# A vision tower on one core: the first group's images loaded at once, pads filled in the opening, maxima spread by one product, the first down integers by two engines, and new orders of work

## The reference

```python
# tokens: quantised patch embedding
xn  = x * rsqrt(mean(x*x) + 1e-6)                       # per patch
xq  = round(xn * s) / s,  s = 127 / clip(max|xn|, 1e-5)
wq  = clip(round(w / clip(mean|w|, 1e-5)), -1, 1) * mean|w|
h   = concat([cls, xq @ wq.T]) + pos                    # (64, 50, 256)

# attention: three sets of weights on the same normed input, 16 heads of 16, causal
for i in range(3):
    q, k, v = (layernorm(h) @ W.T + b for W, b in ((Wq[i], bq[i]), (Wk[i], bk[i]), (Wv[i], bv[i])))
    w = exp(s - max(s)),  s = q @ k.T * 4 with a causal mask
    o = (w / (sum(w) + 1e-6)) @ v @ Wo[i].T + bo[i]
    out[i] = layernorm(o, ln_g[i], ln_b[i])
h = h + layernorm(concat(out) @ Wout.T + bout, ln2_g, ln2_b)

# feed-forward with integers; both maxima run over the WHOLE tensor
y     = layernorm(h);  sx = sigmoid(clip_x) * max|y| / 127
gate  = round(y / sx) * sx @ wq(w_gate).T;  up = the same with w_up   # 704 wide
a     = silu(gate) * up;  sa = sigmoid(clip_down) * max|a| / 127
h     = h + clip(round(a / sa)) * sa @ wq(w_down).T
```

## Time and profile before

| what | value |
|---|---|
| median of 3 runs | 772.16 us (771.97 to 774.45) |
| the profiled execution | 769.84 us, span of its instructions 768.1 us |
| mean granted clock of PE | 0.975 of full speed |
| busy over the span | PE 684.5, DVE 641.9, ACT 584.3, POOL 520.0 us |

### The profile page before, as it was taken

The page is one execution under the profiler, slowest core; times in us unless marked ns, Lnnn a source line. Parts: engine busy times, 40 slices in busy tenths (PEclk is TensorE's granted clock), DMA queues, the critical chain, the costliest instruction groups (busy, mean ns, idle before and its releaser), DMA issues. The chain is left out here.

```text
span 768.1 us, 25770 instructions
## 1 busy us (share of the span) xinstructions
PE 684.5 (89%) x9862; PEld 535.2 (70%) x9862; DVE 641.9 (84%) x1395; ACT 584.3 (76%) x1280; POOL 520.0 (68%) x793
## 2 busy tenths in 40 slices
PE   0498799999999999999999999999999999568866
PEld 0277678777877787877877787788778777334455
DVE  4788876899889988989898899889987898759947
ACT  3567888687788678869778878688868887379875
POOL 3459965957687859877677789478948786521154
PEclk9979999999999999999999999999999999869979
DMA  8301000000000000101000000100100000000005
GB/s 240 100 28 33 17 19 17 19 18 20 4 32 27 10 2 34 34 2 33 18 19 3 16 19 3 34 18 18 41 3 22 20 22 22 1 1 1 0 24 148
DMA packets 14980, 21.95 MB, mean 29 GB/s; under 512 B 1992, under 2 KB 11466, under 8 KB 14860
## 3 DMA queue, kind: packets, MB, share of 16 engines
q1 hardware_dynamic: 14424, 19.91, 8.4%
q10 hardware_dynamic: 436, 0.40, 0.4%
HBM read 17.03 MB, written 3.28 MB: 26 GB/s over the span
## 5 line engine op out<-in xcount | busy, mean ns | idle before, releaser
L905 POOL TENSOR_TENSOR k_bd<-kT,rmask 128x400 f32<-128x400 f32 x192 | 167.8, 902 | 7.5 <-PE ps_s L1358 4.3
L806 ACT COPY pT<-ps_w 25x400 f32<-25x400 f32 x192 | 94.8, 494 | 9.2 <-PE ps_w L1373 6.7
L1399 PE MATMUL ps_w<-oy_hi,o_hi 128*128 128x512 f32 x192 | 94.9, 494 | 0.0
L914 POOL TENSOR_TENSOR prob_hi<-prob_hi,rsum 128x800 f32<-128x800 f32 x48 | 74.9, 1559 | 13.3 <-DVE rsum L1151 13.3
L1134 DVE TENSOR_REDUCE nmax<-ps_s 128x16 f32<-128x400 f32 x96 | 72.4, 765 | 11.6 <-PE ps_s L1358 11.3
L786 ACT COPY v_bd<-ps_w 50x256 f32<-50x256 f32 x192 | 70.4, 367 | 13.2 <-PE ps_w L1333 10.9
L1399 PE MATMUL ps_w<-oy_hi,o_lo 128*128 128x512 f32 x192 | 76.3, 397 | 0.0
L1399 PE MATMUL ps_w<-oy_lo,o_hi 128*128 128x512 f32 x192 | 76.2, 397 | 0.0
L827 ACT ACTIVATE ps_w<-ps_w 128x256 f32<-128x256 f32 x96 | 35.6, 371 | 51.7 <-PE ps_w L1399 50.3
L1358 PE MATMUL ps_s<-k_bd,qT 64*25 64x200 f32 (+1 forms) x3072 | 70.5, 291 | 0.0
L919 POOL TENSOR_TENSOR ln<-ln,ln_eps 128x1 f32<-128x1 f32 x96 | 19.9, 208 | 74.6 <-ACT ps_w L827 74.1
(11 more groups left out here) (237 smaller groups left out, 2070.4 us busy)
## 6 DMA issues: line engine op xcount, KB each, us to landing
x_in<-in_x SPq DMA_DIRECT2D x64, 147.0 KB
out<-hidden SPq DMA_DIRECT2D x14, 200.0 KB
pT<-in_tok_w SPq DMA_DIRECT2D x1, 768.0 KB, 6.5
hidden<-in_wq SPq DMA_DIRECT2D x1, 768.0 KB, 8.6
k_bd<-in_wk SPq DMA_DIRECT2D x1, 768.0 KB, 9.5
v_bd<-in_wv SPq DMA_DIRECT2D x1, 768.0 KB, 9.2
hidden<-in_wout SPq DMA_DIRECT2D x1, 768.0 KB, 9.3
hidden<-in_wo SPq DMA_DIRECT2D x1, 768.0 KB, 10.8
```

The costliest lines, as they stand in the source:

```text
L806: last = nc.scalar.copy(pT[ROWB * h:ROWB * h + LQ, s % 2, c::2, :, 0:LQ], ps_w[row:row + LQ, bank].rearrange("p (j t) -> p j t", j=4)[:, : ...
L905: last = nc.gpsimd.tensor_tensor(k_bd[:, v % KBD, c], kT[:, w % 2, c, 2 * p * L:(2 * p + 2) * L].unsqueeze(1).broadcast_to([P, HR, 2 * L]) ...
L914: nc.gpsimd.tensor_tensor(pr, pr, rsum[:, s % 2, e].unsqueeze(2).broadcast_to([P, H, WIDTH[e]]), ALU.mult).then_inc(prob_ready, 1)
L1399: mm = nc.tensor.matmul(G[:], ot[:, s % 2, c, 2 * (p % 2):2 * (p % 2) + 2].rearrange("p b t -> p (b t)"), wt[:, w, c], start=False, stop=( ...
```

## The change

1. **Loads.** Pairs 2 and 3 of group 0 get places of their own (`x_st`, in memory of `qT` that is not used yet) and are asked for right behind pairs 0 and 1, ahead of the weights. Their squares go to `x_sq` (in `kT`), so a square no longer waits for the rounding buffer. POOL clears the two new places, too. The rows g and b of the last norm are loaded last, by SP.
2. **Pads.** The fills of `prob_lo`, `prob_hi`, `o_hi` and `o_lo` move from the first group's `clear` steps to POOL's opening, before its first step.
3. **k_lo** moves from POOL to DVE.
4. **Maxima.** One product of the column of maxima, broadcast to 128 columns, with the identity leaves the row of maxima on every partition; DVE takes the maximum on all partitions into `mx`. Turn, `one_f` and `top` are gone.
5. **First down integers.** Of group 0's six tiles ACT makes 1, 2 and 3, DVE 0, 4 and 5; of group 1's ACT makes 0, 1 and 2, DVE 3, 4 and 5. The cast of group 0's first half goes from POOL to DVE.
6. **Orders.** The lists of ACT, POOL, DVE and PE are new throughout.

```diff
+    x_st = qT[:].rearrange("p w c t -> p (w c t)")[:, 0:2 * DIN].rearrange("p (j n) -> p j n", j=2)
+    x_sq = kT[:].rearrange("p w c t -> p (w c t)")[:, 0:DIN]
...
+    def x_of(m, p):
+        return x_st[:, p - 2] if m == 0 and p >= 2 else x_in[:, p % 2]
+
+    def x_landed(eng, m, p):
+
+        if m == 0 and p >= 2:
+            eng.wait_ge(x_staged[p - 2], 32)
+        else:
+            eng.wait_ge(x_loaded[p % 2], 64 * m + 32 * (p // 2) + (32 if m == 0 else 0))
...
                 if kind == "sums":
                     p = step[1]
-                    if m == 0 and p < 2:
+                    if m == 0:
                         sp.wait_ge(x_clear, p + 1)
-                    need(sp, xq_ready, PAIRS * m + p - 1)
+                    else:
+                        sp.wait_ge(xq_ready, p + 1 if m == 1 and p < 2 else PAIRS * m + p - 1)
...
-                    nc.scalar.activation(x_t[:], x_in[:, p % 2], ACT.Square, accum_out=xs[:, 0, p:p + 1]).then_inc(sq_ready, 1)
+                    nc.scalar.activation(x_sq if m == 0 else x_t[:], x_of(m, p), ACT.Square, accum_out=xs[:, 0, p:p + 1]).then_inc(sq_ready, 1)
...
             for j in (0, 1):
                 nc.gpsimd.memset(x_in[:, j], 0.0).then_inc(x_clear, 1)
+            for j in (0, 1):
+                nc.gpsimd.memset(x_st[:, j], 0.0).then_inc(x_clear, 1)
...
+            nc.gpsimd.memset(prob_lo[:, :, :, LQ:LQ + 1], SM_EPS)
+            nc.gpsimd.memset(prob_lo[:, :, :, LQ + 1:], 0.0)
+            nc.gpsimd.memset(prob_hi[:, :, :, L:L + 1], SM_EPS)
+            nc.gpsimd.memset(prob_hi[:, :, :, L + 1:], 0.0).then_inc(prob_pads, 1)
+            nc.gpsimd.memset(o_hi[:].bitcast(F32), 0.0)
+            nc.gpsimd.memset(o_lo[:].bitcast(F32), 0.0).then_inc(o_pads, 1)
...
-                if kind == "k_lo":
-                    pool.wait_ge(split_k, 1)
-                    nc.gpsimd.tensor_tensor(qk_lo[:, :, 1], by_row(st_k), qk_hi[:, :, 1].bitcast(F32), ALU.subtract).then_inc(qk_cut, 1)
...
+                if kind == "k_lo":
+                    dve.wait_ge(split_k, 1)
+                    nc.vector.tensor_tensor(qk_lo[:, :, 1], by_row(st_k), qk_hi[:, :, 1].bitcast(F32), ALU.subtract).then_inc(qk_cut, 1)
...
             def find_max(n):
                 pe.wait_ge(y_max if n == 0 else acts_max, 2 if n == 0 else MAXIMA + 1)
-                nc.tensor.transpose(ps_s[0:1, 0, 0, 0:P], mx[:, 2 * n:2 * n + 1], id32[:]).then_inc(max_turned, 1)
-                pe.wait_ge(max_found, n + 1)
-                nc.tensor.matmul(ps_s[:, 0, 1, 0:1], one_f[:], top[:, n:n + 1], start=True, stop=True).then_inc(all_max, 1)
+                nc.tensor.matmul(ps_s[:, 0, 0, 0:P], mx[:, 2 * n:2 * n + 1].broadcast_to([P, P]), id32[:],
+                                 start=True, stop=True).then_inc(max_spread, 1)
...
-            dve.wait_ge(max_turned, 1)
-            nc.vector.tensor_reduce(top[:, 0:1], ps_s[0:1, 0, 0, 0:P], AX.X, ALU.max).then_inc(max_found, 1)
+            dve.wait_ge(max_spread, 1)
+            nc.vector.tensor_reduce(mx[:, 1:2], ps_s[:, 0, 0, 0:P], AX.X, ALU.max).then_inc(max_found, 1)
...
-                    act.wait_ge(hq_ready, 2 * (g - 1) + 2 * T)
-                    for f in range(FC):
+                    if g > 1:
+                        act.wait_ge(first_h, 1)
+                        act.wait_ge(hq_ready, 2 * (g - 1) - 1 + 2 * T)
+                    for f in ((1, 2, 3), (0, 1, 2))[g] if g < 2 else range(FC):
...
+            def h_ints(g, fs):
+                for f in fs:
+                    nc.vector.tensor_scalar(h_int[:, g, f], acts[:, f, g * GT:(g + 1) * GT], hcol[:, 2, f:f + 1], None,
+                                            ALU.mult).then_inc(hint_v_ready, 1)
+            h_ints(0, (0,))
+            dve.wait_ge(hint_v_ready, 1)
+            dve.wait_ge(hint_ready, 2)
+            dve.wait_ge(f_zeroed, 3)
+            nc.vector.tensor_copy(h_q[:, 0, 0:FP, :, 0:L], h_int[:, 0, 0:FP].rearrange("p f (n t) -> p f n t", n=GB)).then_inc(first_h, 1)
+            h_ints(0, (4, 5))
+            h_ints(1, (3, 4, 5))
```

More of the change, by code:

```diff
@@ new lines @@
+        "bo_col": (43,),
+        "sum": (45, 53, 54, 62, 79, 81, 82, 92, 101, 110, 116, 134, 138, 139, 150, 163, 164, 173, 183, 190, 213, 215,
[4 rows of a table added]
+        "z_row": (51, 52,),
+        "fold_lo": (55, 67, 68,),
+        "over": (56, 57, 63, 66, 80, 84, 85, 95, 109, 112, 122, 136, 147, 148, 155, 165, 168, 174, 188, 191, 214,
[4 rows of a table added]
+        "o_lo": (71,),
+        "heads": (86, 87, 104, 105, 132, 154, 170, 189, 195, 206, 234, 251, 275, 287, 303, 304, 337, 357, 366, 386,
+            396, 402, 436, 457, 469, 476, 492, 500, 534, 537, 561, 574, 590, 593, 640, 641, 665, 677, 692, 693, 725,
+            746, 754, 771, 772, 793, 796, 805,),
@@ L264 @@
     "mix": PAIRS, "mix2": PAIRS, "k": NS * KC, "q": NS * KC, "v": S, "heads": S, "spread": V, "project": V,
-    "scores": U, "max": U, "soft": U, "sum": U, "over": U, "turn_p": U,
+    "kbd": S, "scores": U, "max": U, "soft": U, "sum": U, "over": U, "turn_p": U,
 }
@@ L394, in layer @@
     y_in = ybias[0:1]
-    loads = {n: sem("l_" + n) for n in ("ident", "small", "tok", "wq", "wk", "wv", "wo", "wout", "rows_v", "rows")}
+    loads = {n: sem("l_" + n) for n in ("ident", "small", "ln2", "tok", "wq", "wk", "wv", "wo", "wout", "rows_v", "rows")}
     x_clear = sem("x_clear")
@@ L630, in do @@
                     for row, b in HALVES:
-                        sp.dma_start(x_in[row + 1:row + L, p % 2, :], x[m * GB + 2 * p + b]).then_inc(x_loaded[p % 2], 16)
+                        sp.dma_start(x_of(m, p)[row + 1:row + L], x[m * GB + 2 * p + b]).then_inc(
+                            x_staged[p - 2] if m == 0 and p >= 2 else x_loaded[p % 2], 16)
             walk("sp", do)
             for b in (0, 1):
-                sp.wait_ge(x_loaded[b], 64 * GROUPS + 96)
+                sp.wait_ge(x_loaded[b], 64 * GROUPS + 64)
         @block.scalar
         def _(act):
-            for dst, src in ((token0, pos), (g2, ln2_g), (b2, ln2_b)):
-                act.dma_start(dst[:], src.broadcast_to([P, D])).then_inc(loads["small"], 16)
+            act.dma_start(token0[:], pos.broadcast_to([P, D])).then_inc(loads["small"], 16)
             act.wait_ge(pool_up, 1)
@@ L1742, in _ @@
                     for a in (0, 1):
[L1743 removed]
+                        if g == 0 and a == 0:
+                            pe.wait_ge(first_h, 1)
+                        else:
+                            pe.wait_ge(hq_ready, 2 * g + a + 2 * T)
                         for p in range(PAIRS):
```

288 lines of the change are left out of this document (143 added, 145 removed), and 131 rows, old and new, of the table AT.

## The result

The change made the kernel slower: 776.29 us (median of 8 runs, 774.11 to 778.53) against 772.07 (8 runs, 768.65 to 774.45), a ratio of 1.0055 with a 95% interval of 1.0037 to 1.0074. The forecast was 763.3 us with a range of 758.5 to 768.5, so it missed by 13 us and in sign. The profiled execution took 774.11 us, span 772.3; it is compared with the one before, of 769.84 us and span 768.1.

A forecast was written before the change was run, and what follows sets the result against it. The prediction took the attention body to be PE-bound, with the most idle time in the opening. Gains of 6.5 + 0 + 0.8 + 0.7 + 0.9 = 8.9 us against the median 772.16 gave 763.3 us, range 758.5 to 768.5.

The forecast's parts named there:

- New orders in groups 1 to 7: Attention groups 1 to 7: reordered PE steps gain 0, 3 us to either side; bounds 12 gained and 12 lost.
- Rival 4: Groups 1 to 7: a step too early in an in-order list makes PE wait each time; slower, 777 at 2 us a group; chance 0.06.
- The opening, 6.5: First 100 us: earlier loads and first k product, less moved work and holes, gain 6.5 us; best 10, worst -1.
- 4 us of holes: Behind the first k product, to the old 100 us mark: PE idle for 4 us, where it was 6.1.
- The 41.0 for k: Opening: first k product starts at about 41.0 us, 9.4 earlier, range 40.5 to 43.5.
- rival 1: Opening: earlier k start only moves work, PE keeps its slack; opening gains 3.1 us, time 766.7; chance 0.18.
- the low start of k: Opening: k may start at the low clock level, since transposes don't count as work; at most 3 us worse.
- My price for it: Opening: 1 us for a half clock in the first k products, bounds 0 and 3.
- End of attention, 0.8: Last group: heads 1.9 us earlier, DVE gives 1.2 back; net 0.8 us gained, bounds 2 gained and 1 lost.
- Two maxima, 0.7: Both maxima: one spreading product replaces turn, maximum and spreading; 0.4 and 0.3 us gained, together 0.7.
- first down integers, 0.9: First down product: ACT and DVE share the integers and DVE casts, so PE starts 0.9 us earlier (0.7 to 1.1).

The follow-up runs named there:

- The part alone: The kernel before with only the two maxima and the first down integers changed: 769.91 us, ratio 0.997 (0.9941 to 0.9999).

## Why the prediction was wrong

**The step that failed.** It is the one under "New orders in groups 1 to 7": "Nothing in the rows says which way a reshuffle goes. I take 0 with 3 us to either side, a quarter of what is idle". From the mark of group 1 to the last large turns the changed kernel takes 9.8 us more than the one before, and the new lists from group 1 to group 7 alone, put between old ones, cost about 11 (about 7 by the price above, without seams). The bound in the same paragraph, 12 lost, held; the central value and the 3 us did not. That PE had little idle time to give and much to lose should have moved the value off 0: PE was idle for only 12.2 of 540 us. That most reshuffles lose from there is my reading; what the runs show is that every kernel with new lists in some stretch was slower than the one with none. Rival 4 had the right place. Its price was set at 1.6 us a group to turn the sign, since it had 8.9 us to eat; a mean of 1 us a group did it because the opening did not pay either. Its mechanism was half right. PE's idle time from 100 to 640 us grew by 6.9 us; waits for DVE, summed over the view of waits, went from 8.4 us in 17 to 12.7 in 27, none above 1.24, waits for POOL from 0.7 to 2.0, and idle time with no semaphore from 1.7 to 2.9. That is many small waits, as before, and most of the added ones in groups 5 and 6, rather than one step in every group.

**The opening, 6.5.** The load times, the first k product (0.96 us late) and the idle time before 100 us were right, and still the mark of group 1 (before 123.7) came only 2.2 to 2.6 us earlier, with the new orders (121.1) as with the old ones (121.5), in whose list k starts 5.5 us later. What failed is the step from "idle time saved" to "time gained": behind the first k product I counted PE's work and allowed 4 us of holes. PE's busy time to 100 us grew by 5.9 us (65.3 to 71.2) with 13 instructions fewer. Part of this is the low clock of 43.3 to 46.5 and 57.5 to 67.4 us; but with the holes filled PE waits for DVE until the same time (63.56 against 63.37). DVE was busy for 22.3 of the 24.1 us from 43.3 to 67.4 us. A collision with POOL such as the one in the kernel before stood in no term of the sum (only the range for k allowed for one), and no one-column DVE step of 2 us was left, as forecast, but one of 1.61 was. The 41.0 for k was in part luck: pair 3's statistics end at 34.97, 1.7 us ahead of the 36.7 forecast, and DVE's steps that lasted longer beside POOL (1.86 in place of 0.41 for a norm at 35.99, and q's low part) took that back and 1 us more. It is close to rival 1 (PE's gain is only moved), and it should have had more than 0.18; I had its argument, DVE's added 2.7 us, on the page. The early loads themselves are worth 3.3 us at the mark under the old orders. Of the 13 us missed the opening is 3.9 (2.6 in place of 6.5).

**On the clock.** I had left open whether k would start at the lower level, by the rule of the Trainium skill, page "TensorE: Matmul & The Clock Gate", section "Part 4: PE-mode transpose", that transposes do not count as work for the clock. k started at 2.4 GHz and fell to 1.2 at 43.3 us, 2 us behind the hole of 2.99. In the run with filled holes the same turns ran and the clock stayed up. So the low start of k that I had read from the rule did not come, and filling the holes was enough to keep the clock up, with the turns left as they were; whether turns alone would hold it down, no run here shows. My price for it, 1 us with a bound of 3, covered the first stretch and missed the second, of 9.9 us.

**End of attention, 0.8.** The heads waited 0.62 in place of 2.27, as forecast (less than 1.5), and the section is 2.0 us shorter, at my bound of 2. But the run with only the new end was 4 us slower than the old orders, gaps and seam included, so this gain did not show in the time.

**Two maxima, 0.7, and first down integers, 0.9.** 0.4 and 0.1 for the maxima (the second took 1.16, before 1.26, where I had 1.0), 0.9 for the integers: 1.4 against 1.6, and 1.0 between the cuts. The part alone gave 0.3% (0.01 to 0.59%). Right in mechanism and size.

**What stays open.** Why the new lists of groups 5 and 6 make PE wait. It is not one late DVE step (moving four made it worse), not DMA (18 and 19 GB/s), and in the changed kernel only in small part the gaps with no semaphore (2.9 us, before 1.7). What brings these gaps, and how much of a seam's cost is theirs, stays open too.

## What to carry to other kernels

Where an order of work is already tuned, treat new lists as a change of their own and time the structural edits under the old lists first: here these were 0.8 to 0.9% faster (765 us, the fastest kernel of this study), and shipping both together hid it. The list of an engine that is busy for 98% of a stretch (527.8 of 540.0 us here) has more to lose from a reshuffle than to gain; a forecast of 0 with even bounds is then a bias. When a kernel is cut into stretches to find a cost, sum up the idle time that no semaphore explains first, and do not charge it to the stretch. And an early start of a bound engine is worth only what the engine that feeds it can follow: check the feeder's busy time behind the start, not the hole before it.

## What the hardware showed that I had not expected

A hole of 2.2 us in PE's work (54.75 to 56.95) was followed by about 10 us at 1.2 GHz, and one of 2.99 by 3.2 us; filling the holes with products that nothing reads kept 2.4 GHz through them and gained nothing.

A DVE step can last several times as long beside a POOL step: 1.61 us in place of 0.16 on one column, and 3.19 in place of 1.73 on 1536, where POOL's steps took 1.64 and 1.67.

PE can stand for up to 2.3 us in the middle of 128 small products with no semaphore to wait for, at the same product in four kernels (the 89th), and in another place (1.76 us) with no data transfer beside it. So the place can be the same in several kernels, but whether and how long PE stands changes between two executions of one kernel (none and 0.95 us near 555 us). The page lists a queue of its own for instructions (80 packets, 1.31 MB over the span); that it has to do with the gaps is a guess.
